# Turning the input of a grouped convolution with VectorE instead of TensorE and GpSimd

## The reference

```python
c   = conv(x, weight (32, 8, 9), pad 4, 4 groups) + (cond @ c_weight.T)[:, :, None] + bias[None, :, None]
up   = c @ W_up.T            # c as rows of 512, W_up is (1376, 512)
gate = silu(c @ W_gate.T)    # W_gate is (1376, 512)
out  = x + (gate * up) @ W_down.T
```

## Time and profile before

| | |
|---|---|
| median of 3 runs | 769.61 us (767.9 to 770.84) |
| the profiled execution | 767.56 us |
| its span in the trace | 765.5 us |
| TensorE clock granted, mean over the span | 0.994 of full speed |
| TensorE matmul busy | 749.1 us, 98% |
| VectorE / ScalarE / GpSimd busy | 56% / 36% / 11% |

### The profile page before, as it was taken

How to read it: one execution, slowest core, us unless ns; L and a number is a source line. 1 busy time by engine, 2 the same in 40 slices (tenths; PEclk the granted TensorE clock), 3 DMA queues, 4 the chain that set the end, 5 groups by cost and what they waited for, 6 DMA issues and landing times.

```text
span 765.5 us, 10216 instructions
## 1 busy us (share of the span) xinstructions
PE 749.1 (98%) x3465; PEld 611.8 (80%) x3465; DVE 428.8 (56%) x701; ACT 275.7 (36%) x519; POOL 82.6 (11%) x113
## 2 busy tenths in 40 slices
PE   7789999999999999999999999999999999999997
PEld 6567888878888888887888888887788888887886
DVE  4787767665674555556744555555753444445223
ACT  3565554543442332324421333233431233333220
POOL 4434242310000110000100010100000000000000
PEclk9999999999999999999999999999999999999999
DMA  6687667688987687777444877768443866666413
GB/s 197 193 291 261 231 229 260 216 269 284 370 284 252 182 251 214 216 233 215 143 142 150 290 208 223 219 217 247 139 141 108 299 196 193 193 193 177 138 27 111
DMA packets 116564, 160.75 MB, mean 210 GB/s; under 512 B 9922, under 2 KB 47970, under 8 KB 116514
## 3 DMA queue, kind: packets, MB, share of 16 engines
q1 hardware_dynamic: 116320, 160.02, 66.0%
q10 hardware_dynamic: 194, 0.08, 0.0%
HBM read 117.34 MB, written 42.73 MB: 209 GB/s over the span
## 4 chain that ended last, share of the span: by engine, by line
PE 94%; DMA 2%; DVE 1%; ACT 1%; issue 1%; SPq 0%; ACTq 0%; DVEq 0%
PE bank L703 54%; PE bank L766 31%; PE bank L616 2%; PE bank L621 2%; PE bank L596 2%; DMA turned<-g_all 1%; PE bank L659 1%; DVE hc_lo L1059 1%; PE bank L630 1%; DMA stage<-turned 0%; PE bank L641 0%; DMA g_all<-in_cond 0%; DVE g_all L1270 0%; ACT hc_hi L835 0%; PE bank L578 0%
## 5 line engine op out<-in xcount | busy, mean ns | idle before, releaser
L703 PE MATMUL bank<-hc_hi,ring 128*128 128x512 f32 (+1 forms) x1204 | 377.3, 394 | 3.0 <-DVE ring L1059 2.2
L703 PEld LDWEIGHTS bank<-hc_hi,ring 128*128 128x128 f32 (+1 forms) x1204 | 220.7, 186 | 51.6 <-DVE ring L1059 2.5
L703 PE MATMUL bank<-hc_lo,ring 128*128 128x512 f32 (+1 forms) x602 | 235.8, 392 | 0.0
L766 PE MATMUL bank<-ring,g_hi 128*128 128x512 f32 (+1 forms) x704 | 218.6, 392 | 0.1
L766 PEld LDWEIGHTS bank<-ring,g_hi 128*128 128x128 f32 (+1 forms) x704 | 131.2, 188 | 28.3 <-DVE g_lo L1059 0.8
L835 ACT ACTIVATE mix<-bank 128x512 f32<-128x512 f32 (+1 forms) x129 | 77.1, 598 | 212.0 <-PE bank L703 212.0
L766 PE MATMUL bank<-ring,g_lo 128*128 128x512 f32 (+1 forms) x352 | 137.1, 390 | 0.0
L703 PEld LDWEIGHTS bank<-hc_lo,ring 128*128 128x128 f32 (+1 forms) x602 | 111.8, 186 | 26.3
L1059 DVE TENSOR_TENSOR g_lo<-g_all,g_hi 128x512 fp32r<-128x512 f32 (+1 forms) x88 | 60.9, 695 | 83.7 <-ACT g_hi L835 83.7
L835 ACT ACTIVATE g_hi<-g_all 128x512 fp32r<-128x512 f32 (+1 forms) x88 | 55.1, 629 | 114.0 <-PE bank L766 114.0
L1236 DVE TENSOR_TENSOR mix<-bank,mix 128x512 f32<-128x512 f32 (+1 forms) x43 | 29.7, 691 | 94.6 <-ACT mix L953 94.6
(11 more groups left out here) (141 smaller groups left out, 546.5 us busy)
## 6 DMA issues: line engine op xcount, KB each, us to landing
ring<-saved SPq DMA_DIRECT2D x319, 256.0 KB, 2.9
saved<-ring SPq DMA_DIRECT2D x99, 256.0 KB, 2.4
stage<-turned SPq DMA_DIRECT2D x32, 256.0 KB, 3.3
g_all<-in_x SPq DMA_DIRECT2D x32, 256.0 KB, 3.7
out_y<-g_all SPq DMA_DIRECT2D x32, 256.0 KB, 3.4
x_in<-in_x SPq DMA_DIRECT2D x13, 512.0 KB, 4.6
turned<-win SPq DMA_DIRECT2D x12, 512.0 KB, 4.5
w_nat<-in_L_ffn_W_gate SPq DMA_DIRECT2D x10, 256.0 KB, 4.4
```

The lines of the kernel that those rows point to most:

```text
L703: mm = pe.matmul(bank[0:w, :], wt, hv, start=fresh and q == 0 and t == 0, stop=q == 1 and t == 2, skip_group_check=not fresh)
L766: mm = pe.matmul(acc(half, tt)[:], gs, wd, start=f == 0 and t == 0, stop=f == FC - 1 and t == 2)
```

## The change

- For groups 1 to 3, `load_x` issues eight DMAs of 64 KB in place of one of 512 KB. They lay the channels out so that turning squares of 32 by 32 is enough: partitions 32q to 32q+31 hold channels 2q and 2q+1 of all 128 sequences.
- VectorE turns 128 x 512 elements into `x_turn` (the memory of `x_blk`) with one `transpose`, `turn_x(g+1, k)`, the first instruction of its step, ahead of `gate_a`.
- `split_x` reads `x_turn` in SBUF in place of the bank, for these groups.
- TensorE's `turn_x` and GpSimd's `block_x` are left for group 0 alone.
- SP's waits ahead of `load_x` are now on `x_turned` with a count one step later in the same numbering: the load of the next two steps waits for VectorE's turn `k+1`, which is the first instruction of VectorE's step `f+1`.
- The channels now come out in another order, so the filter's Toeplitz pieces of groups 1 to 3 are reordered once: a permuted identity made by GpSimd, three float32 matmuls of 192 columns (`reorder_toep`, after `product(0, 1, 1)`, with a wait for `g_done[1]`), two copies by ScalarE.
- The wait on `y_added` that TensorE's `turn_x` had moves to `conv_head`.

```diff
+        x_turn = x_blk[:, :, :, :].rearrange("n b r c -> n (b r c)")
...
             def load_x(grp, i):
+                if grp > 0:
+                    for quad in range(NB):
+                        for c in range(CQ):
+                            sp.dma_start(x_in[quad * QUAD:(quad + 1) * QUAD, c::CQ, :],
+                                         x[:, grp * CG + quad * CQ + c, i * P:(i + 1) * P].rearrange("(b n) l -> n b l", b=NB)
+                                         ).then_inc(x_loaded, LD)
+                    return
...
                     if g + 1 < G and k in (0, 2, 4):
-                        sp.wait_ge(x_blocked, STEPS * (g + 1) + k + 1)
+                        sp.wait_ge(x_turned, STEPS * (g + 1) + k + 2)
                         load_x(g + 1, k // 2 + 1)
...
                 if g + 2 < G:
-                    sp.wait_ge(x_blocked, STEPS * (g + 2) - 1)
+                    sp.wait_ge(x_turned, STEPS * (g + 2))
                     load_x(g + 2, 0)
...
-                    if g + 1 < G and f == 0:
-                        block_x(g + 1, 0)
...
-                    if g + 1 < G and lag(g) <= f < STEPS - 1 + lag(g):
-                        block_x(g + 1, f + 1 - lag(g))
...
+            def reorder_toep():
+
+                pe.wait_ge(toep_done, 2)
+                pe.wait_ge(consts, 9)
+                pe.wait_ge(xt_lo_done, STEPS)
+                pe.wait_ge(g_done[1], 1)
+                for grp in range(1, G):
+                    to = conv_ps if grp == G - 1 else xt_ps
+                    at = (grp - 1) % 2 * QN * CG
+                    mm = pe.matmul(to[:, at:at + QN * CG], reorder[:], toep[:, grp, :, :], start=True, stop=True)
+                mm.then_inc(toep_mm, 1)
...
-                    if conv and 0 <= k < STEPS:
-                        turn_x(g + 1, k)
+                    if g == 0 and k == 0:
+                        reorder_toep()
...
+                if grp == 1:
+                    act.wait_ge(toep_mm, 2)
+                    hi(toep[:, 1:G - 1, :, :], xt_ps[:, 0:(G - 2) * QN * CG].rearrange("p (g q o) -> p g q o", g=G - 2, o=CG))
+                    hi(toep[:, G - 1, :, :], conv_ps[:, 0:QN * CG].rearrange("p (q o) -> p q o", o=CG)).then_inc(toep_done, 1)
+                    act.wait_ge(toep_done, 3)
...
+            def turn_x(grp, k):
+                dve.wait_ge(x_loaded, LD * CG * (KC * (grp - 1) + k // 2 + 1))
+                if grp == 1 and k == 0:
+                    dve.wait_ge(x_turned, STEPS)
+                else:
+                    dve.wait_ge(xt_lo_done, STEPS * grp + k)
+                l0 = k % 2 * WB * R
+                dve.transpose(x_turn, x_in[:, :, l0:l0 + WB * R].rearrange("p m (w r) -> p w m r", r=R)).then_inc(x_turned, 1)
...
                     last = f == FC - 1
+                    if conv and 0 <= k < STEPS:
+                        turn_x(g + 1, k)
                     gate_a(n, f)
```

More of the change, by code:

```diff
@@ L119, in adaln_ffn @@
             up1 = sb("up1", [P, TOK], F32R, early)
+            reorder = sb("reorder", [P, P], F32, early)
         g_hi = sb("g_hi", [P, NG, TOK], F32R)
@@ L296, in copy_block, with x_split_from @@
                  .rearrange("n c (b r) -> n b r c", r=R)).then_inc(x_blocked_first if grp == 0 and k == 0 else x_blocked, 1)
+        QUAD = 32
+        NB, CQ = P // QUAD, CG // (P // QUAD)
+        x_turn = x_blk[:, :, :, :].rearrange("n b r c -> n (b r c)")
+        def x_split_from(grp, k):
+            return xt_bank(grp, k)[:] if grp == 0 else x_turn
         def xt_at(grp, k):
@@ L329, in load_x @@
             def load_x(grp, i):
+                if grp > 0:
[5 more added lines that the diff above has]
+                    return
                 sp.dma_start(x_place(grp, i), x[:, grp * CG:(grp + 1) * CG, i * P:(i + 1) * P]
-                             ).then_inc(x_first_loaded[i] if grp == 0 else x_loaded, LD)
+                             ).then_inc(x_first_loaded[i], LD)
             def load_nat(f):
@@ L481, in block_x @@
             def block_x(grp, k):
[L482 to L488, removed]
+                pool.wait_ge(x_first_loaded[k // 2], LD)
+                if k > 1:
                     pool.wait_ge(x_turned, k - 1)
@@ L532, in _ @@
             block_x(0, 7)
+            pool.wait_ge(consts, 8)
+            pool.tensor_copy(reorder[:].rearrange("p (m r) -> p m r", r=R), ident[:].rearrange("p (r m) -> p m r", r=R)).then_inc(consts, 1)
             wrap(1)
@@ L582, in turn_x @@
             def turn_x(grp, k):
-                if grp == 0 and k == 0:
+                if k == 0:
                     pe.wait_ge(x_blocked_first, 1)
+                    pe.wait_ge(conv_w_ready, 1)
                 else:
[L586 to L589, removed]
+                    pe.wait_ge(x_blocked, k)
+                if k > 1:
                     pe.wait_ge(xt_lo_done, k - 1)
[L591 to L594, removed]
                 for b in range(WB):
@@ L597, in turn_x @@
                 mm.then_inc(x_turned, 1)
+            def reorder_toep():
[8 more added lines that the diff above has]
+                mm.then_inc(toep_mm, 1)
             def conv_head(grp):
+                if grp > 1:
+                    pe.wait_ge(y_added, 2 * OB * (grp - 1))
                 pe.wait_ge(t_lo_done, grp + 1)
@@ L849, in split_x @@
                 at = xt_at(grp, k)
-                last = hi(xt(grp)[0][:, at:at + WB * P], xt_bank(grp, k)[:])
+                last = hi(xt(grp)[0][:, at:at + WB * P], x_split_from(grp, k))
                 if grp > 0 and k % 2 == 0 and k > 0:
-                    last = hi(xt_hi[:, 2 * WB * P:], xt_bank(grp, k)[:, 0:P])
+                    last = hi(xt_hi[:, 2 * WB * P:], x_turn[:, 0:P])
                 last.then_inc(xt_hi_done, 1)
@@ L1101, in split_x @@
                 at = xt_at(grp, k)
-                last = lo(xt(grp)[1][:, at:at + WB * P], xt_bank(grp, k)[:], xt(grp)[0][:, at:at + WB * P])
+                last = lo(xt(grp)[1][:, at:at + WB * P], x_split_from(grp, k), xt(grp)[0][:, at:at + WB * P])
                 if grp > 0 and k % 2 == 0 and k > 0:
-                    last = lo(xt_lo[:, 2 * WB * P:], xt_bank(grp, k)[:, 0:P], xt_hi[:, 2 * WB * P:])
+                    last = lo(xt_lo[:, 2 * WB * P:], x_turn[:, 0:P], xt_hi[:, 2 * WB * P:])
                 last.then_inc(xt_lo_done, 1)
```

## The result

The changed kernel takes 777.5 us (median of 4 runs, 775.49 to 778.74), the kernel before beside it 769.37 (4 runs, 767.9 to 770.84): a ratio of 1.0094, interval 1.0072 to 1.0115. The forecast was 777.6. The profiled execution took 777.15, with a span of 775.3, against 767.56 and 765.5 before.

The account below looks back on a forecast made before the run. TensorE, busy 98% of the span, was taken as the bound. Turns and small additions gave -8.2 us, late-store waits +13.0, clock +3.2: +8.0 on 767.56, 777.6 as a median; range 761 to 788, the forecast's own 773 to 786.

Parts of the forecast that it names:

- The turns: TensorE's transposes on line 596 for groups 1 to 3 go: 23 turns of 0.43 us count, 9.9 us off.
- the rival of a slow turn: VectorE's turn takes 1.2 us, lengthening all six waits and making `xt_lo` late beside group 0: 784.9 us; chance 0.10.
- Beside group 0: VectorE's denser list there makes the even steps' `xt_lo` 0.2 us late, four times: 0.8 us added.
- Issues: SP's queue: eight load issues at 0.45 us each, 3.6 us together, ahead of the store of `win`; bounds 0.32 and 0.53 each.
- the landing: Store of `win` lands 4.5 us after issue (median; 3.6 to 5.8), 4.0 beside group 0; VectorE's `read_conv` needs it.
- The waits: TensorE's `product` 6 held by the late store: 2.6 us four times, 1.3 twice beside group 0, 13.0 us added.
- The first rival: Store late by less with issues of 0.38 us, and the clock holds: 771.0 us; chance 0.25.
- the forecast with all six: TensorE's clock falls behind all six waits, 1.6 us each, 9.6 in all; used for the range's upper end, 788.
- The rival in which the store keeps its cover: SP's eight issues take under 1.0 us together, the store lands by 8.1, only -8.2 us remain: 761.4; chance 0.18.
- The clock: TensorE's granted clock falls behind two of four 2.6 us waits, 1.6 us each: 3.2 us added, bounds 0 and 9.6.
- The start: One more VectorE pass where TensorE stood still, 0.6 us, and the reordering matmuls in TensorE's 2.24 us hole, 0.3 us.
- The sum: -8.2 + 13.0 + 3.2 = +8.0 us on the profiled 767.56, so 775.6; as a median 777.6.

Follow-up runs that it names:

- e5_store_first_turn_in_gap: The version with both moves: changed kernel with store of `win` ahead of the load, and each turn but a group's first in VectorE's gap one step earlier; 757.85 us, ratio 0.9827.
- e1_store_first: Changed kernel with SP's store of `win` issued ahead of the wait for VectorE's turn and the eight loads, nothing else; 758.88 us, ratio 0.984.
- e3_one_issue: Changed kernel with one 512 KB load in place of eight, old layout (output wrong), still behind the wait for VectorE's turn; 760.53 us, ratio 0.9864.
- e7_sixteen_issues: Changed kernel with each of the eight loads cut into two of 32 KB; 808.46 us, ratio 1.0504.
- e6_turn_in_gap_only: Changed kernel, SP's order unchanged, each turn but a group's first moved between `up_b` and the silu of the step before; 761.54 us, ratio 0.9885.
- e4_before_eight_issues: Kernel before with its load cut by channel into eight DMAs of 64 KB, TensorE and GpSimd keeping the turn; 768.04 us, ratio 0.9968.
- a1_after_again: Changed kernel unchanged, measured again beside the kernel before, on the chip of the sixteen-issue run; 775.92 us, ratio 1.0072.
- e2_before_store_first: Kernel before with its store of `win` ahead of the load and its wait, nothing else; 768.85 us, ratio 0.9985.

## Why the prediction was right

**The turns.** Right in kind, a little low in size. A step beside groups 1 and 2 without a store wait went from 11.39 us (`gate_a` at 261.05 and 272.44 before) to 10.94 (268.50 and 279.44 after): 0.45, where the prediction had 0.43; in the version with both moves such steps are 0.46 to 0.49 shorter than before. VectorE's turn took 0.71, at the low end of the 0.6 to 1.2, so the rival of a slow turn is out. The estimate from the Trainium skill's "VectorE: DVE Perf Modes", section "The three transpose paths", was 1.24 us for it; the trace has little more than half, for a turn in squares of 32 by 32 and in float32, where the page's figure is for bf16.

**Beside group 0.** Right, though the changed kernel's own profile hides it, since its waits lie in odd steps. `e1_store_first` has the same turns without the waits: there the even steps (`k` = 2, 4, 6) shrink by 0.26 or 0.27 and the odd ones (`k` = 3, 5) by 0.49, where 0.23 and 0.43 were forecast. Only `k` = 1 is off, by 0.32. With the turn in the gap all seven shrink by 0.41 to 0.48, so it was the place of the turn ahead of the split that cost the even steps their part.

**Issues.** Right, and this decided it: 3.65 for eight, 3.6 predicted; sixteen of half the size took 7.46. The chain from there came out like this beside group 1, in us after zero:

| | predicted | measured |
|---|---|---|
| SP goes on | 2.65 | 2.55 |
| store issued | 6.25 | 6.51 |
| store landed, `read_conv` starts | 10.75 | 10.14 |
| `up_b` done | 12.05 | 11.43 |
| TensorE waits | 2.6 | 2.05 |

The one term of this chain off in size is the landing: 3.6 us there, where the median of before, 4.5, was taken; in all of the changed kernel it is 3.5 / 3.9 / 5.1. The runs show a pattern in it. Beside groups 1 and 2 `read_conv` starts 5.4 to 5.9 us after the store's issue in the kernel before and 4.8 to 5.1 in `e3_one_issue`, where one load of 512 KB is issued just ahead of the store. Where eight or sixteen small loads were issued ahead of it, over 3.65 us and more, it is 3.6 to 4.1 in the changed kernel, 3.5 to 3.7 in `e7_sixteen_issues`, 3.6 to 4.0 in `e6_turn_in_gap_only` and 3.6 to 4.7 in `e4_before_eight_issues`. So the median of all twelve stores stood for neither case, and the longer issuing gave part of its delay back in a quicker landing. Whether the size of the pieces or the time between them does it was not separated. The waits came to 12.5 against 13.0: four of 2.05 to 2.30 in place of 2.6, and beside group 0 2.42 and 1.19 in place of 1.3 each. The 2.42 is the first one, where the eight issues took 4.89:

```profile
97.06 4.89 SPq L343 DMA_DIRECT2D x_in<-in_x  x8
102.26 0.39 SPq L398 DMA_DIRECT2D turned<-win  x1
```

**The first rival** had waits of 2.05 beside groups 1 and 2, close to what came, but by shorter issues (0.38, where they took 0.46) and not by a quicker landing; beside group 0 it had 0.7, and no clock loss. Two bounds of the prediction were added up wrongly: the upper end of the waits comes to 28.7 and not 28, and the forecast with all six falls to 784.0 and not 788. Neither bears on the forecast.

**The rival in which the store keeps its cover** needed issues of under 1.0 us for all eight. The Trainium skill's "DMA: Bandwidth & Descriptors", section "Anatomy of one DMA — SWDGE (gpsimd) path", would give 0.4 for the dispatch of eight; SP's queue shows nine times that, so its figure did not carry over from the path it speaks of. `e1_store_first` then gave this rival's cover back by order in place of speed, and the kernel was faster, at 758.88 where the rival had 761.4.

**The clock.** The mechanism was right, the number a matter of the execution: two of four falls were taken; one of six came in the first profile, three of six in `a1_after_again`. What the prediction didn't have is that a wait without a fall also costs some 0.25 us more than it lasts, as said at `e7_sixteen_issues`. Its reason for counting two of four was also read too loosely: ahead of the wait of 2.24 us TensorE had done transposes from 49.38 on, 0.8 us of them, but dense matmuls up to there.

**The start.** VectorE's chain ahead of step 1 grew by the 0.6 us that one more pass was put at, but the profile's start differs by more, for another reason (below). TensorE then waited 2.58 us at 65.02, where it had waited 0.78, and ran at a clock of 0.79 from 64 to 72, where it had 1.00: some 2 us that the prediction did not have. This too belongs to that one execution and not to the change. In `a1_after_again` and `e1_store_first` the clock falls near 56 us, as it did at 53 before, TensorE waits 0.99 there, and no fall follows; `gate_a` comes again after 13.41 and 13.42 us in place of 15.02. The early fall costs nothing, since TensorE waits behind it anyway: `up_b` of step 1 starts 7.71 us after `gate_a` with it (`a1_after_again`) and 7.70 without it (the first profile).

**The sum** came out closer than its terms, and that is luck. From `gate_a` of step 2 to the last `gate_a` the kernel before takes 628.45 us, `e1_store_first` 617.74: 10.7 less (0.4 of it because a turn stands ahead of the first `gate_a` and not of the last), where the prediction's terms for this stretch, 22 turns of 0.43 less 0.8, make 8.7. The changed kernel takes 633.03 there, 15.3 more than `e1_store_first`: 12.5 of waits, about 1.5 for one fall, and 0.25 behind each of the other five. By the medians both terms are too small. The change without the delay is worth 12.6 us (771.49 to 758.88), where the prediction had 8.2; not all of that is in the steps, and what is left stays open. The delay costs 18 to 20 us by the ratios (1.0072 and 1.0094 against 0.984), where it had 16.2 (13.0 and 3.2). The two errors cancel for the most part. The mechanism and its sign are shown; the last microsecond is not, as the second measurement has the change at 4.9 us over the kernel before (775.92 and 771.02) and the first at 8.1.

**What I sized too low in the experiments.** `e1_store_first` was to take 763.5 and took 758.88, 18.6 under the changed kernel and 17.0 under its second measurement. I had reckoned with the waits and one fall, 14.0. From `gate_a` of step 1 to the last one, the profile of `e1_store_first` takes 631.16 us, the changed kernel's 648.05, 16.9 more: 12.5 of waits, 2.8 behind them (one fall and five times 0.25), 1.6 for the fall near 66. `a1_after_again` takes 649.94, 18.8 more: 12.7 of waits and 6.1 behind them, with three falls. So the medians' 17.0 to 18.6 is what one to three falls give; how often each number comes was not counted. `e3_one_issue` and `e5_store_first_turn_in_gap` were worked out from the same base and came out 5.0 and 4.5 low with it.

## What to carry to other kernels

On a queue that runs in order, put what somebody soon waits for ahead of what waits itself: here one store behind a wait and eight issues turned a gain of 1.6% into a loss of 0.9%. A DMA cut in n pieces cost its queue n issues here, 0.46 us each at 64 KB and at 32 KB, and that counts when something urgent stands behind them. Two delays that each fit in a slack must be summed: what remains of it is read from the time of landing against the time of need, not from whether anyone waits today. And a forecast that comes out right is checked term by term: here two terms were some 2 to 4 us too small, with opposite signs.

## What was not expected

TensorE's clock comes up at a different time from one execution to the next, before TensorE has come to anything of the change. These are rows of TensorE's timeline of the kernel before, then of the kernel after, at the same kind of matmul in the setup:

```profile
11.20 0.40 PE L621 MATMUL bank<-hc_hi,tb_hi 128*128 128x512 f32 x1
```

```profile
12.99 0.63 PE L640 MATMUL bank<-hc_hi,tb_hi 128*128 128x512 f32 x1
```

A matmul of 512 columns lasts 0.40 at the full clock and 0.63 at half (the granted clock's column does not show it this early). Before, the full pace was there from 8.9 us on; after, from some 15 on. The profiles of `e2_before_store_first` and `e5_store_first_turn_in_gap` have it as early, those of the other runs only at some 13 to 15 us, `e4_before_eight_issues` among them, so it goes with neither kernel. At 22 us this had put the changed kernel's profiled execution 2.86 us behind, nearly a third of the 9.8 between the two spans. Medians of executions, not one against one, carry a verdict of a per cent here; the kernel before itself ranged over 767.65 to 773.24 us in 13 runs on one chip.

How little a wait of 2 us on TensorE costs, or how much, is likewise a draw: behind waits of 2.42 and 2.05 us the matmuls above came at half and at full clock. In `a1_after_again` the clock fell behind waits of 2.15, 2.28 and 2.72 us and held behind 2.02 and 2.37; behind the six waits of 5.5 to 6.0 us in `e7_sixteen_issues` it always fell.
